# Four normalisations and the rows between edge maxima made chunk by chunk inside the node products, the next round's weights loaded during the maxima, the output stored by chunks

## The reference

```python
def _layernorm(x, axis=-1, eps=1e-05):
    m = jnp.mean(x, axis=axis, keepdims=True)
    v = jnp.var(x, axis=axis, keepdims=True)
    return (x - m) / jnp.sqrt(v + eps)
```

```python
        def _edge_conv(x, src, dst, W1, b1, W2, b2, n_nodes):
            xi = x[dst]
            xj = x[src]
            m = jnp.concatenate([xi, xj - xi], axis=-1)
            h = jax.nn.relu(m @ W1 + b1) @ W2 + b2
            agg = jax.ops.segment_max(h, dst, num_segments=n_nodes)
            return jnp.where(jnp.isfinite(agg), agg, 0.0)
```

## Time and profile before

| | |
|---|---|
| median of 3 runs | 12301.65 us (12288.66 to 12314.6) |
| profiled execution, its own time | 12306.0 us |
| span of its trace | 12304.2 us |
| TensorE busy (matmuls) | 7391.4 us, 60% |
| VectorE busy | 7065.6 us, 57% |
| GpSimd busy | 6720.9 us, 55% |
| ScalarE busy | 2531.9 us, 21% |
| DMA | 1436.26 MB, mean 117 GB/s |
| granted clock of TensorE, mean | 0.754 |

### The profile page before, as it was taken

How to read it: one execution, slowest core, us unless ns; L and a number is a source line. 1 busy time by engine, 2 the same in 40 slices (tenths; PEclk the granted TensorE clock), 3 DMA queues, 4 the chain that set the end, 5 groups by cost and what they waited for, 6 DMA issues and landing times. The chain is left out here.

```text
span 12304.2 us, 181472 instructions
## 1 busy us (share of the span) xinstructions
PE 7391.4 (60%) x39114; PEld 6245.1 (51%) x39115; DVE 7065.6 (57%) x13587; ACT 2531.9 (21%) x8694; POOL 6720.9 (55%) x6703
## 2 busy tenths in 40 slices
PE   4944444366665677636444443637777677767776
PEld 4944444355554555524344443635555555555554
DVE  6844444433345888866754545675555555555555
ACT  2500000011110000046400000322333233323332
POOL 0088888366642666523236664316666466646665
PEclk7966666555557888879867666768898888888888
DMA  4356556322213666545324443313333334433433
GB/s 118 72 95 96 96 96 97 88 65 65 66 51 93 210 211 213 192 99 157 104 83 127 131 129 103 113 47 129 131 131 132 110 133 132 132 109 132 132 130 121
DMA packets 828886, 1436.26 MB, mean 117 GB/s; under 512 B 183440, under 2 KB 494844, under 8 KB 788336
## 3 DMA queue, kind: packets, MB, share of 16 engines
q1 hardware_dynamic: 531712, 981.94, 25.6%
q0 software_dynamic: 297072, 453.23, 16.7%
HBM read 1115.44 MB, written 320.07 MB: 117 GB/s over the span
## 5 line engine op out<-in xcount | busy, mean ns | idle before, releaser
L1612 POOL DMA_INDIRECT T<-gather_d,srci x2508 | 2516.5, 1003 | 1604.1 <-issue 652.4
L1198 PE MATMUL PS<-T 128*128 x3328 | 1045.0, 404 | 1072.3 <-DVE T L1214 824.1
L838 POOL DMA_INDIRECT added_d<-T,slots x832 | 1292.1, 1553 | 288.4 <-issue 224.1
L920 DVE TENSOR_TENSOR T<-T,PS 128x128 f32 (+1 forms) x2092 | 560.3, 287 | 1465.4 <-remote 1064.7
L1198 PEld LDWEIGHTS PS<-T 128*128 128x128 f32 x3328 | 710.6, 244 | 1223.1 <-issue 1169.7
L1149 POOL DMA_INDIRECT T<-wide_d,srci x832 | 832.6, 1001 | 738.4 <-PEq L71 287.1
L1149 POOL DMA_INDIRECT T<-gather_d,srci x832 | 825.6, 992 | 677.4 <-PEq L71 239.5
L943 POOL DMA_INDIRECT T<-gather_d,srci x832 | 799.8, 961 | 643.3 <-DVE T L1014 265.5
L1731 DVE TENSOR_TENSOR_SCAN T<-T,PS 128x512 f32<-128x512 f32 x624 | 798.1, 1279 | 597.7 <-remote 362.9
L1420 PE MATMUL PS<-T 128*128 128x260 f32 (+1 forms) x3328 | 801.0, 400 | 423.6 <-DVEq L1473 370.0
L1656 PE MATMUL PS<-T,W 128*128 128x512 f32 x1248 | 828.2, 751 | 350.8 <-ACT T L1692 190.2
(11 more groups left out here) (248 smaller groups left out, 14708.2 us busy)
## 6 DMA issues: line engine op xcount, KB each, us to landing
T<-quads_d SPq DMA_DIRECT2D x315, 1024.0 KB
T<-edge_rows_d SPq DMA_DIRECT2D x210, 512.0 KB
edge_rows_d<-T SPq DMA_DIRECT2D x209, 512.0 KB
T<-onehot_t_d SPq DMA_DIRECT2D x416, 256.0 KB
T<-gather_d,srci POOLq DMA_INDIRECT x4172
T<-edge_rows_d SPq DMA_DIRECT2D x210, 256.0 KB
onehot_t_d<-T SPq DMA_DIRECT2D x208, 256.0 KB
edge_rows_d<-T SPq DMA_DIRECT2D x208, 256.0 KB
```

The source lines that it names most:

```text
L838: gp.indirect_dma_start(added_d[u][:, :], bass.IndirectOffsetOnAxis(ap=slots[:, k:k + 1], axis=0), part(OUT[r], u), None, compute_op=ALU.a ...
L1198: T_.matmul(spot(i, u), part(OT[r], u), T2[:, bass.ds(bs[i * GROUP + u] * width, width)], start=True, stop=False)
L1612: gp.indirect_dma_start(part(R[n % RING], u), None, gather_d[:, :], bass.IndirectOffsetOnAxis(ap=srci[:, k:k + 1], axis=0)).then_inc(rows_ ...
```

## The change

`layernorm()` and `give_back()` go. `node_linear()` gets two optional arguments:

- `norm`: the normalisation of `X` into `H` is done inside the block. VectorE centres the seven chunks (reduce, scale, subtract); ScalarE squares the first five chunks with an accumulated sum, block by block (35 activations of 128x128); VectorE squares and sums chunks 5 and 6; then come one scaling, root and reciprocal for all 49 blocks (in a new small buffer `spread`), and `ready(j)`: relu and scaling of a chunk in one pass of VectorE. TensorE's transposes of chunk j wait for `ready(j)`. All four layers use it.
- `before`: a function that makes a chunk's rows. Rounds two and three of layer 3 use it for what VectorE did over whole tables after the maxima: two additions and one fused relu and multiplication, per chunk.

VectorE's order in the block is ready(0), and then for each chunk j: ready(j + 1), the additions of chunk j. An output without `add` is a copy in place of an addition; layer 3's first output uses it, and the zero bias and its memset go. In layer 3 the weights alternate between two halves of `W`: SyncE issues the loads for the next round at the start of `edge_maxima()` and waits for them at its end. In layers 1 to 3 the first load of weights now stands ahead of the normalisation. After the last round VectorE makes the output in 7 chunks of four passes, and SyncE stores each when it is made.

The new parts of `node_linear()`:

```diff
                     def transposes(j):
+                        if fed:
+                            pe.wait_ge(rows_ready.h, rows_ready.at(j + 1))
...
+                    def square(j):
+                        act.wait_ge(centred.h, centred.at(j + 1))
+                        for u in range(NB):
+                            last = S_.activation(norm(j)[:, u * DIM:(u + 1) * DIM], mine(H, j)[:, u], ACT.Square,
+                                                 accum_out=spread[:, j * NB + u:j * NB + u + 1])
+                        last.then_inc(squared.h, 1)
+
+                    if norm is not None:
+                        for j in range(by_scalar):
+                            square(j)
+                        act.wait_ge(vv_done.h, vv_done.at(1))
+                        S_.activation(spread[:, :], spread[:, :], ACT.Sqrt).then_inc(ac_done.h, 1)
...
+                    def centre(j):
+                        x, mean = mine(X, j), of_chunk(small, j)
+                        c.link(V.tensor_reduce(mean, x, AX.X, ALU.add))
+                        c.link(V.tensor_scalar(mean, mean, 1.0 / DIM, None, ALU.mult))
+                        V.tensor_tensor(mine(H, j), x, each(mean, DIM), ALU.subtract).then_inc(centred.h, 1)
+
+                    def ready(j):
+                        if norm is not None:
+                            h = mine(H, j)
+                            V.scalar_tensor_tensor(h, h, 0.0, each(of_chunk(spread, j), DIM), ALU.max, ALU.mult).then_inc(rows_ready.h, 1)
+                        elif before is not None:
+                            before(c, j).then_inc(rows_ready.h, 1)
+
+                    if norm is not None:
+                        for j in range(chunks):
+                            centre(j)
+                        for j in range(by_scalar, chunks):
+                            dve.wait_ge(centred.h, centred.at(j + 1))
+                            q = norm(j).rearrange("p (u w) -> p u w", w=DIM)
+                            c.link(V.tensor_tensor(q, mine(H, j), mine(H, j), ALU.mult))
+                            c.link(V.tensor_reduce(of_chunk(spread, j), q, AX.X, ALU.add))
+                        dve.wait_ge(squared.h, squared.at(by_scalar))
+                        V.tensor_scalar(spread[:, :], spread[:, :], 1.0 / DIM, 1e-5, ALU.mult, ALU.add).then_inc(vv_done.h, 1)
+                        dve.wait_ge(ac_done.h, ac_done.at(1))
+                        c.link(V.reciprocal(spread[:, :], spread[:, :]))
+                    ready(0)
                     for j in range(chunks):
+                        if j + 1 < chunks:
+                            ready(j + 1)
                         for n, o in enumerate(outs):
```

Layer 3 and the end:

```diff
+            def maxima_of(c, n, j):
+
+                part_of = lambda tab: tab[:, j * NB * DIM:(j + 1) * NB * DIM].rearrange("p (u w) -> p u w", w=DIM)
+                m, h = part_of(T1[:, ROWS:2 * ROWS]), part_of(H)
+                c.link(V.tensor_tensor(m, m, h, ALU.add))
+                c.link(V.tensor_tensor(m, m, every(at(n, 4), NB), ALU.add))
+                return m, h, each(has[:, j * NB:(j + 1) * NB], DIM)
+
+            def difference(c, n):
+                c.link(V.tensor_tensor(at(n, 0), at(n, 0), at(n, 1), ALU.subtract))
+
+            def next_rows(n):
+                def rows(c, j):
+                    if j == 0:
+                        difference(c, n)
+                    m, h, there = maxima_of(c, n - 1, j)
+                    return V.scalar_tensor_tensor(h, m, 0.0, there, ALU.max, ALU.mult)
+                return rows
+
+            load_weights(weights(0))
...
+            for n in range(3):
+                node_linear([(H, DIM, 0)], [dict(w=[at(n, 1)], to=(T1[:, ROWS:2 * ROWS], DIM, 0), store=gather_d),
+                                            dict(w=[at(n, 0)], add=at(n, 3), to=(T1, DIM, 0))], T2,
+                            norm=None if n else lambda j: T2[:, ROWS + j * NB * DIM:ROWS + (j + 1) * NB * DIM],
+                            before=next_rows(n) if n else None)
+                edge_maxima(at(n, 2), weights(n + 1) if n < 2 else [])
...
+                    for j in range(BLOCKS // NB):
+                        m, _h, there = maxima_of(c, 2, j)
+                        x = X[:, j * NB * DIM:(j + 1) * NB * DIM].rearrange("p (u w) -> p u w", w=DIM)
+                        c.link(V.tensor_tensor(m, m, there, ALU.mult))
+                        V.tensor_tensor(x, x, m, ALU.add).then_inc(rows_ready.h, 1)
+
                 @block.sync
                 def _(sp):
-                    full = NODES // P
-                    sp.dma_start(out[0:full * P, :].rearrange("(t p) f -> p t f", p=P), blocks(X, DIM)[:, 0:full]).then_inc(stored.h, 16)
+                    for j in range(BLOCKS // NB):
+                        b0, b1 = j * NB, min((j + 1) * NB, full)
+                        sp.wait_ge(rows_ready.h, rows_ready.at(j + 1))
+                        sp.dma_start(out[b0 * P:b1 * P, :].rearrange("(t p) f -> p t f", p=P), blocks(X, DIM)[:, b0:b1]).then_inc(stored.h, 16)
```

More of the change, by code:

```diff
@@ L429, in build, with node_linear @@
         bias_row = lambda ap, n=DIM: ap.rearrange("(a n) -> a n", a=1)[0:1, 0:n].to_broadcast([P, n])
[L432 removed]
+        def node_linear(srcs, outs, stage, norm=None, before=None):
             K, n_out, chunks = len(srcs), len(outs), BLOCKS // NB
@@ L490, in _ @@
                                 src = to
-                            last = V.tensor_tensor(to, src, every(o["add"], NB), ALU.add)
+                            last = V.tensor_tensor(to, src, every(o["add"], NB), ALU.add) if o.get("add") is not None else V.tensor_copy(to, src)
                             if o.get("relu"):
@@ L1777, in layer3, with weights @@
         def layer3():
[L1778 to L1779 removed]
+            names = ("in", "hid", "out")
+            at = lambda n, k: wcol(5 * (n % 2) + k)
+            def weights(n):
+                name, o = names[n], 5 * (n % 2) * DIM
                 w1 = I[f"L3_W1_{name}"]
[L1782 to L1805 removed]
@@ new lines, in difference, with _ @@
+            def difference(c, n):
[8 more added lines that the diff above has]
+            load_weights(weights(0))
+            with nc.Block() as block:
+                @block.vector
+                def _(dve):
+                    difference(vch.on(dve), 0)
@@ new lines, in layer3, with _ @@
+            with nc.Block() as block:
+                @block.vector
+                def _(dve):
+                    c = vch.on(dve)
+                    for j in range(BLOCKS // NB):
[3 more added lines that the diff above has]
+                        V.tensor_tensor(x, x, m, ALU.add).then_inc(rows_ready.h, 1)
```

89 lines of the change are left out of this document (25 added, 64 removed).

## The result

| | before | the change |
|---|---|---|
| median | 12301.65 us (12288.66 to 12314.6) | 12374.5 us (12369.37 to 12384.24, 5 runs) |
| ratio | | 1.0059, 95% interval 1.0045 to 1.0074 |
| span of the profiled execution | 12304.2 us | 12378.9 us |

The account below looks back on a forecast made before the run. No engine is over 60% busy; VectorE's chains ahead of node products and TensorE in them bound it. -71.2 + 48.6 + 2 x (-1.7) - 6.1 + 45 = +12.9 us, giving 12314.6 us on the median; range 12269 to 12340 us.

Parts of the forecast that it names:

- The first transpose 22.9 us after the first reduce: Normalisation ahead of each node product: first transpose at 22.9 us instead of 40.6, -17.7 us per layer, -70.8 over four.
- ScalarE's squares at nothing: Normalisation: ScalarE's 35 squares cost no time, ending near 13.7 us against 20.7 on VectorE.
- some 6 us before it: Normalisation: sign that ScalarE's last square comes some 6 us before the first transpose.
- The new wait: Node products: transposes wait behind VectorE's additions, 2.43 us a cycle (+48.6), 4.67 in rounds two and three (+23.4 each).
- The clock: Node products: TensorE's clock lapses after gaps, 1.7, 0.9 or 1.9 us lost per burst, +45 us in all.
- The end: Output passes and store: passes +3.6 us, last chunk's store -9.5, block boundary -0.3, together -6.1 us.
- rival A: Node products: TensorE's clock holds through the gaps, -32.1 us, 12269.5 us; chance 0.15.
- B: Node products: TensorE's clock stays low, each of 30 bursts loses 2.6 us, +78 instead of +45, 12347.6 us; chance 0.13.
- C: Node products: the passes are hidden, chunks keep TensorE's pitch or VectorE's 5.4 us, -109 us, 12192 us; chance 0.03.
- Sum.: Whole kernel: the terms add to +12.9 us, taking the profiled execution from 12306.0 to 12318.9 us.

Follow-up runs that it names:

- pass_1792: The kernel before plus a block with one VectorE product over 1792 columns ahead of layer 2's wide gathers: ratio 1.0004 on the quick chip, 1.0019 on a slower.
- pass_1: The kernel before plus a block with one VectorE product over 1 column ahead of layer 2's wide gathers: ratio 1.0002 on the quick chip, 1.0019 on a slower.
- ready2: The change with VectorE making rows ready two chunks ahead instead of one: 12359.81 us, ratio 0.9956 to the kernel before.
- norm_apart: The change with the normalisation of layers 0 to 2 put back as passes of its own before the node product: 12423.62 us, ratio 1.0008 to before.
- ready2_pass: The change with rows ready two chunks ahead, plus a one-column VectorE product block ahead of the wide gathers: ratio 0.9897 on the quick chip, 0.9952 on a slower.
- ready2_placed: ready2 with 78 and 102 one-column VectorE memsets under the weight loads ahead of and behind layer 1's edges: 12351.6 us, ratio 0.9936 to before.
- two_blocks: The kernel before with two more blocks, each a single small VectorE memset, ahead of layer 1 and of layer 2: 12452.54 us, ratio 1.0031.
- one_dve: The kernel before with one memset of 1 column added on VectorE in layer 2's normalisation: 12326.54 us, ratio 1.0027.

## Why the prediction was wrong

**Right.** "The first transpose 22.9 us after the first reduce": 22.95. ScalarE's squares at nothing: they end 13.8 us after the first reduce (forecast 13.7), and ScalarE idles 5.80 us ahead of the root. (The sign "some 6 us before it" fits that idle time; before the first transpose, by the prediction's own figures, it is 9.2, and was 9.1.) The new wait of 2.43 and 4.67 us a cycle, five cycles a product: TensorE idles 2.18 and 4.43 ahead of the transposes. The clock: 1.6 us lost in a turn of round two, 1.9 assumed; layer 0's five turns average 6.0 us and layer 1's 6.3 where 4.8 would be without a loss, 1.2 and 1.5 lost, 1.7 assumed; in layer 2 and in layer 3's first product 0.5 and 0.7, 0.9 assumed. The end -6.2, forecast -6.1. Together +11.0 for +12.9. That on the chip without stalls the whole kernel shows +3 to +23 us is in part luck: there too an unedited stage, the second weighted sums, took 10 us more (515.5 against 505.4 and 505.6 in pass_1792 and pass_1). Neither rival A nor B was needed, and ready2 shows that C's price was right and that the order of the two engines was what barred it.

**Wrong** was the step "**Sum.** -71.2 + 48.6 + 2 x (-1.7) - 6.1 + 45 = +12.9 us. The profiled execution took 12306.0 us, span 12304.2, and gives 12318.9". It carries over 10.9 ms of edge stages as a constant, because no line of theirs is edited. Nothing in the text prices that or gives it a range; the only scatter in it is that of one program's own runs, which is no measure of how a stage differs between two programs. In place of 0 it was +64 in the profiled pair (68 in the long stages, less the 4.4), some +53 on chip 3 (64.5 us by the medians, less the 11 of the edited stretches), and little on the quick chip (11.5 us by the medians, less the same 11; in the traces the ten long stages are 15 to 16 us longer than in pass_1 and pass_1792, but the change's profiled execution is the slowest of its eleven).

How much of it has a shown cause: the wide gathers and the second weighted sums, +42 of 68, and the cause is shown as far as the engine whose instruction stream does it. In the wide gathers, +33, one added VectorE instruction gives the same stage, rhythm and loss; one on ScalarE or TensorE, unused names, or a later entry does not. The change moves 72 instructions into VectorE's stream ahead of that loop, and put back as they were (norm_apart) the stage is quick. The second weighted sums, +9, took 515.4 to 515.8 us in all six traces of the change, ready2 and ready2_pass, on both kinds of chip, and 505.1 to 507.4 in all others, norm_apart and ready2_placed among them; the second differs from ready2 in VectorE's stream alone, but for a buffer. Layer 1's edges (+18, and 1345 to 1349 in three traces of the change and its variants against 1323 to 1337 in seven of the others on chips near 12300) and the second maxima (+10) fit the same account and were not isolated. For layer 1's edges it is weaker: on chip 1 two_blocks left them as they were, and ready2 took 1379.9 against 1372.6 to 1375.6. Open is by what rule the place counts, and why TensorE's semaphores rise late on the slower chips. That the place acts through the fetching of instructions is a guess, and the traces speak against a fetch in each turn: the wide gathers see ten instruction packets on queue 14 and one on queue 8 in every trace, of either rhythm and on every chip.

The trace of before did hold a warning: in its layer 1 edges VectorE idles for 532 of 1331 us in stalls that the profile puts down to nothing near their end (the L920 row above), and TensorE's semaphore of that stage rises 156 times where 208 increments were made. A stage whose bound can't be named should not have been carried as a constant.

## What to carry to other kernels

Where stages are loops of several engines whose long waits the trace can't name, allow in the forecast for such a stage to take another rhythm: here 0.6 us a turn, up to 33 us a stage, from one instruction on one engine. Before blaming an edit for a loss, cut both traces at the block borders, and see whether the loss lies where the edit is. When rows are made chunk by chunk for a product, make them two chunks ahead: the order sum, rows, transposes, products cost all that the fused passes had saved, and with the rows one chunk earlier the kernel was 0.4 to 1.0% faster than before.

## What was not expected of the hardware

- The same program took 11130 us on one chip and 12295 to 12430 us on four others. Stages without gathers take the same on every chip within some 3% (layer 0's edge weights 393.5 to 393.8 everywhere); the six with GpSimd's gathers differ (layer 1's edges 1065 to 1070 against 1323 to 1386). So a ratio of two kernels, too, holds for a kind of chip: 1.0012 on the one, 1.0051 and 1.0059 on two others.
- On the slower chips the wide gathers settle into one of two rhythms, 24.7 or 25.2 to 25.5 us a turn in the mean: the first in all six programs whose VectorE stream is that of before up to there, the second in all nine others traced on such chips.
- On the slower chips semaphores that TensorE's products raise show up late and merged: 132 to 169 rises for 208 increments in layer 1's edges and 147 to 166 in the wide gathers, against 207 to 209 on the quick chip.
- The Trainium skill (Trainium Architecture — The Big Picture, The software stack) says that the instruction streams are moved into each engine's memory when the program is loaded. The traces show more than that: 71 instruction packets of 8 KB on queue 14 during the execution of before and of one_dve, and 74 in the change's, so part of the stream still comes in while it runs.
